# Grouped attention on one Trainium2 core: scores and values of a key tile alternate by halves in TensorE's order

## The chip, the cores and the metric

The program runs on one core of a Trainium2 chip, in one launch. The metric is the device time of that launch in microseconds. A core has a matrix engine (TensorE, PE in the rows, with its weight loads as PEld), a vector engine (DVE), a scalar engine (ACT), GpSimd (POOL) and DMA queues. Each engine runs its own instruction stream in program order; streams meet only through semaphores.

## The reference, cut to what matters

Two layers are computed on `x` (4 x 256 x 512) with a context of 4 x 1601 x 512. Layer 0 is a latent cross attention and an int4 linear layer; layer 1 is the attention below and a mixture of low-rank experts. The change is in the attention of layer 1:

```python
hidden = concatenate([context, latents], axis=1)          # 1601 + 256 = 1857 keys
q = (latents @ Wq.T)   # 16 heads of 96
k = (hidden @ Wk.T)    # 4 key-value heads of 96, each for G = 4 query heads
v = (hidden @ Wv.T)
scores = einsum('bkgqd,bksd->bkgqs', q, k) / sqrt(96)
attn = softmax(scores)
out = einsum('bkgqs,bksd->bkgqd', attn, v) ... @ Wo.T
x = x + out
```

## The kernel before, in words

Four stages follow each other: `context_products`, `latent_attention_and_ffn`, `grouped_attention` and `mixture`. Only the third, `grouped_attention`, is changed. Queries, keys and values come to it through DRAM.

It loops over S = 16 heads s (4 batches x 4 key-value heads). A head has 4 query heads x 256 queries = 1024 query columns, held as two halves of 512 (one PSUM bank each), and KT = 15 key tiles kt of 128 keys, the last of 65. All products are made from a high and a low part, three matmuls each:

- `scores(s, kt)`: for each half, three matmuls into one of SB = 3 score banks (L1435 to L1437). Each bank waits until ACT is done with what stood in it three halves before (`exp_done`).
- ACT, `probs`: for each half two exponentials of the same bank, `ph` (L1530, the high part) and `pf` (L1533, full precision). `pf` waits for POOL to be done with the same half of the tile before.
- POOL subtracts, `pl = pf - ph` (L1366), the low part, once per half.
- `values(s, kt)`: for each half, three matmuls into the output bank of that half (L1452, L1453 with `ph`; L1455 with `pl`). They accumulate over the 15 tiles; at the first tile of the next head they wait for `o_done`, the two copies by which ACT empties both output banks (L1557). ACT issues these copies behind `probs(s + 1, 0)` in its stream, and they wait for the last `values` of head s.

Beside it runs a ring of other work, `ring_item`, in the order that `beside(s)` writes out: for head s + 1 the 32 products of queries and keys whose row maxima DVE takes (L1383, read by L1605), the sum of head s - 1 (L1387, L1607), its 8 output projections (L1394 to L1396, read by L1610), and after each batch a layer norm on DVE (L67 to L82, heads 5, 9 and 13; it has two ring items between its Newton passes L77 to L79) and the first products of the mixture. A ring item takes one of RB = 3 banks and waits until DVE has read what stood there three items before. `fill()` on TensorE issues the next ring item, if there is one left. DVE takes the items in the same order.

The row maxima of head s + 1 are needed before its first scores: at kt = KT - 2, `max_rows(s + 1)` transposes them on TensorE (L1422), DVE writes them into the query operand (`rows_of`, L93), and `scores(s + 1, 0)`, issued at kt = KT - 1, waits for that (`row_done`).

TensorE's order for one key tile is, with S for the scores of the next tile, V for the values of this one, f for a ring item and 0 and 1 for the halves: `S0 f S1 f V0 f V1 f`. In the last three tiles (`late`) no item stands behind V; and S of the last tile is that of the next head's first, without items. The items of a normal head run out at kt = 10, those of heads 5, 9 and 13 at kt = 12; head 15 has none in its first 12 places. The streams of ACT, POOL and DVE are not touched by the change.

Of the kernel before, what the change touches and what calls it, by code (L numbers as in the profile page):

```python
# [14 lines left out]
BANK = 512  # L15
# [8 lines left out]
H1, KV1, HD1 = 16, 4, 96  # L24
# [1157 lines left out]
def grouped_attention(nc, A, ident, negid, ps, ln, q_scr, k_scr, v_scr, x_scr, y_scr, z_scr, wo_scr, w1T, h8all, dlall):  # L1182
# [5 lines left out]
    S = B * KV1  # L1188
    KT = KT1
# [7 lines left out]
    with ExitStack() as ctx:  # L1197
        def sb(name, shape, dt=F32):
            return ctx.enter_context(nc.sbuf_tensor(name, shape, dt))

        def sem(name):
            return ctx.enter_context(nc.semaphore(name))

        kf = sb("kf", [HD1, NK])
        kh = sb("kh", [HD1 + QT, 3, NK + 1], F32R)
        kl = sb("kl", [HD1, 3, NK + 1], F32R)
        vf = sb("vf", [P, KT, HD1])
        vh = sb("vh", [P, 2, KT, HD1 + 1], F32R)
        vl = sb("vl", [P, 2, KT, HD1 + 1], F32R)
        qh = sb("qh", [HD1 + QT, 3, GC], F32R)  # L1210
        ql = sb("ql", [HD1, 3, GC], F32R)
        woT = sb("woT", [HD1, 2, G, D], F32R)
        ph = sb("ph", [P, 2, GC], F32R)
        pl = sb("pl", [P, 2, GC], F32R)
# [22 lines left out]
        s_mm, phi, exp_done, plo = sem("scores1"), sem("probs_hi"), sem("probs1"), sem("probs_lo")  # L1237
        av_mm, o_done, n_done = sem("values1"), sem("o_copied1"), sem("x_normal")
# [3 lines left out]
        OB, M0, RB, SB = 3, 5, 3, 3  # L1242

        def bank(i, n=BANK):
            return ps[:, i * BANK:i * BANK + n]
# [30 lines left out]
        def read(kind, a, i):  # L1276

            return ring_done, ring[kind, a, i] + 1
# [90 lines left out]
        @block.tensor  # L1369
        def _(pe):  # L1370
            def ring_item(kind, a, i):
                n = ring[kind, a, i]
                at = bank(M0 + n % RB)
                if n >= RB:
                    pe.wait_ge(ring_done, n - RB + 1)
                if kind == "max":
                    if i == 0:
                        pe.wait_ge(q_in[a % 3], 32 * (a // 3 + 1))
                    j, ch = i // len(cuts), i % len(cuts)
                    k0, _, k = cuts[ch]  # L1380
                    if j == 0:
                        pe.wait_ge(kh_done, 4 * a + ch + 1)
                    mm = pe.matmul(at[:, 0:k], qh[0:HD1, a % 3, j * P:(j + 1) * P], kh[0:HD1, a % 3, k0:k0 + k],  # L1383
                                   start=True, stop=True)
                elif kind == "sum":
                    pe.wait_ge(sum_in, (a + 1) * 16)
                    mm = pe.matmul(at[:, 0:QT], sums[:, :], ident[0:QT, 0:QT], start=True, stop=True)  # L1387
                elif kind == "out":
                    if i == 0:
                        pe.wait_ge(wo_in, 16 * (a + 1))  # L1390
                        pe.wait_ge(ol_done, a + 1)
                    h, t = i // TT, i % TT
                    cols = slice(h * T + t * P, h * T + (t + 1) * P)
                    pe.matmul(at, oh[:, cols], woT[:, 0, h, :], start=True, stop=False)  # L1394
                    pe.matmul(at, oh[:, cols], woT[:, 1, h, :], start=False, stop=False)
                    mm = pe.matmul(at, ol[:, cols], woT[:, 0, h, :], start=False, stop=True)  # L1396
                elif kind == "turn":
                    if i == 0:
                        pe.wait_ge(n_done, a + 1)
                    for c in range(2):  # L1400
                        for t in range(TT):
                            mm = pe.transpose(at[:, c * T + t * P:c * T + (t + 1) * P],
                                              xn[:, t, (2 * i + c) * P:(2 * i + c + 1) * P], ident[:, :])
                elif kind == "h":
                    if i == 0:
                        pe.wait_ge(*read("turn", a, 1))
                    for c in range(DC):
                        mm = pe.matmul(at, xT[:, c, i * P:(i + 1) * P], w1T[:, c, :], start=(c == 0), stop=(c == DC - 1))
                elif kind == "z":
                    for c in range(DC):  # L1410
                        mm = pe.matmul(at[0:R, 0:T], aw[:, c, :], xT[:, c, :], start=(c == 0), stop=(c == DC - 1))
                elif kind == "h8":
                    for c in range(DC):
                        mm = pe.matmul(at[:, 0:NE], xT[:, c, 1:T:2], w1T[:, c, 0:NE], start=(c == 0), stop=(c == DC - 1))
                else:
                    pe.wait_ge(*read("z", a, 0))
                    mm = pe.matmul(at[:, 0:NE], zb[:, 1:T:2], liT[:, :], start=True, stop=True)
                mm.then_inc(ring_mm, 1)

            def max_rows(s):  # L1420
                pe.wait_ge(mxr_done, s + 1)
                pe.transpose(bank(M0)[0:QT, 0:P], mx[:, :], ident[:, :]).then_inc(row_mm, 1)  # L1422

            def scores(s, kt, fill):
                n = s * KT + kt
                if kt == 0:
                    pe.wait_ge(row_done, s + 1)
                    pe.wait_ge(kl_done, 4 * s + 4)
                k0, m = kt * P, keys[kt]
                for half in range(2):  # L1430
                    if 2 * n + half >= SB:
                        pe.wait_ge(exp_done, 2 * n + half - SB + 1)
                    out = bank((2 * n + half) % SB)[0:m, :]
                    cols = slice(half * BANK, (half + 1) * BANK)
                    pe.matmul(out, kh[:, s % 3, k0:k0 + m], qh[:, s % 3, cols], start=True, stop=False)  # L1435
                    pe.matmul(out, kl[:, s % 3, k0:k0 + m], qh[0:HD1, s % 3, cols], start=False, stop=False)  # L1436
                    mm = pe.matmul(out, kh[0:HD1, s % 3, k0:k0 + m], ql[:, s % 3, cols], start=False, stop=True)  # L1437
                    mm.then_inc(s_mm, 1)
                    if half == 0:
                        fill()  # L1440

            def values(s, kt, fill):
                n = s * KT + kt
                if kt == 0:
                    pe.wait_ge(vl_done, 4 * s + 4)
                    if s:
                        pe.wait_ge(o_done, 2 * s)
                m = keys[kt]
                for half in range(2):
                    out, cols = bank(OB + half)[0:HD1 + 1, :], slice(half * BANK, (half + 1) * BANK)  # L1450
                    pe.wait_ge(phi, 2 * n + half + 1)
                    pe.matmul(out, vh[0:m, s % 2, kt, :], ph[0:m, n % 2, cols], start=(kt == 0), stop=False)  # L1452
                    pe.matmul(out, vl[0:m, s % 2, kt, :], ph[0:m, n % 2, cols], start=False, stop=False)  # L1453
                    pe.wait_ge(plo, 2 * n + half + 1)
                    mm = pe.matmul(out, vh[0:m, s % 2, kt, :], pl[0:m, n % 2, cols], start=False, stop=(kt == KT - 1))  # L1455
                    if half == 0:
                        fill()
                mm.then_inc(av_mm, 1)

            pe.wait_ge(const, 5)  # L1460
            for item in beside(-1):
                ring_item(*item)
            max_rows(0)
            pe.wait_ge(w_small, 48)
            for s in range(S):
                items = iter(beside(s))

                def fill():
                    item = next(items, None)
                    if item:  # L1470
                        ring_item(*item)

                if s == 0:
                    scores(0, 0, lambda: None)
                for kt in range(KT):
                    if kt + 1 < KT:
                        scores(s, kt + 1, fill)
                        fill()
                    elif s + 1 < S:
                        scores(s + 1, 0, lambda: None)  # L1480
                    if s + 1 < S and kt == KT - 2:
                        max_rows(s + 1)
                    late = kt > KT - 4
                    values(s, kt, (lambda: None) if late else fill)
                    if not late:
                        fill()
                assert next(items, None) is None
            for item in beside(S) + last_batch():
                ring_item(*item)
# [349 lines left out]
```

## Time and profile before

| | us |
|---|---|
| runs | 2040.28, 2049.16, 2047.75 (median 2047.75) |
| profiled execution | 2043.46, of it span 2041.7 |
| TensorE busy | 1922.5 (94% of the span) |
| ACT, DVE, POOL busy | 944.3, 1118.8, 653.1 |

The span holds all four stages. Busy time is a sum over the stages, so that what a change in the third is worth has to be read in a timeline of the third. In that, each row is one instruction (or several in a row): start, duration, engine, line, operation, tiles. A matmul's row is longer than the distance to the next one, because they are pipelined; the distance between starts is what it costs. Brackets at a row's end give the idle time of its engine before it and what ended that.

### The profile page before, as it was taken

The numbers are of one execution on the slowest core, as the hardware profiler recorded it, in microseconds if no ns is written. First come the engines' busy times: TensorE is split into PE (matmuls) and PEld (weight loads), VectorE is DVE, ScalarE is ACT, GpSimd is POOL, SyncE is SP. The second block draws the span as 40 slices with busy tenths as digits, with TensorE's granted clock in tenths as the row PEclk, the third lists the DMA queues.
The fourth block names the chain that finished last, engine by engine and source line by source line (L and its number), as shares of the span: only waits on it lengthen the run. The fifth ranks groups of instructions, "written<-read, shape, count | busy, mean of one in ns | idle before, by whom it ended". The sixth has DMA issues, their size and how long they took to land. (4 is left out here: it accounts for less than half of the span.)

```text
span 2041.7 us, 23682 instructions
## 1 busy us (share of the span) xinstructions
PE 1922.5 (94%) x8690; PEld 1368.1 (67%) x8690; DVE 1118.8 (55%) x2093; ACT 944.3 (46%) x1826; POOL 653.1 (32%) x504
## 2 busy tenths in 40 slices
PE   6999998999999999998869999999999999999986
PEld 6999984444555556464637777767777777777752
DVE  1433325666666665652266666666666566664433
ACT  1332322444344334343127666655666466665640
POOL 0000000000000000000028777756776577765740
PEclk9999995999899999999769999999999999999996
DMA  5556733000111010010261232213222222212112
GB/s 176 157 170 204 226 121 70 1 11 17 50 34 42 31 42 27 11 52 26 80 167 45 75 85 75 60 30 86 74 72 75 76 79 62 56 49 57 31 31 97
DMA packets 109697, 149.51 MB, mean 73 GB/s; under 512 B 28777, under 2 KB 87529, under 8 KB 106510
## 3 DMA queue, kind: packets, MB, share of 16 engines
q1 hardware_dynamic: 101630, 145.36, 24.9%
q10 hardware_dynamic: 7952, 2.64, 0.6%
q8 instruction: 69, 1.13, 0.2%
q14 instruction: 46, 0.38, 0.1%
HBM read 96.52 MB, written 51.39 MB: 72 GB/s over the span
## 5 line engine op out<-in xcount | busy, mean ns | idle before, releaser
L1366 POOL TENSOR_TENSOR pl<-pf,ph 128x512 fp32r<-128x512 f32 (+1 forms) x480 | 640.9, 1352 | 300.9 <-ACT pf L1533 299.2
L1530 ACT ACTIVATE ph<-ps 128x512 fp32r<-128x512 f32 (+1 forms) x480 | 288.5, 601 | 352.8 <-PE ps L1437 351.8
L1605 DVE TENSOR_REDUCE pm<-ps 128x1 f32<-128x464 f32 (+1 forms) x512 | 317.9, 635 | 119.9 <-PE ps L1383 113.5
L1132 DVE TENSOR_REDUCE pm<-ps 128x1 f32<-128x400 f32 (+1 forms) x512 | 264.2, 567 | 103.1 <-PE ps L970 100.2
L1031 ACT ACTIVATE pr<-ps 128x512 f32<-128x512 f32 (+1 forms) x416 | 219.4, 602 | 194.3 <-PE ps L909 193.0
L1533 ACT ACTIVATE pf<-ps 128x512 f32<-128x512 f32 (+1 forms) x480 | 289.2, 603 | 0.2 <-POOL pl L1366 0.2
L1355 POOL MEMSET vf<- 128x96 f32 x1 | 0.2, 178 | 711.2 <-POOLq L685 711.2
L1383 PE MATMUL ps<-kh,qh 96*128 96x464 f32 (+1 forms) x512 | 199.6, 399 | 21.9 <-DMA ql<-q_scr 12.9
L922 PE MATMUL ps<-pr,cv 128*64 128x512 f32 (+1 forms) x832 | 208.1, 616 | 0.0
L1435 PE MATMUL ps<-qh,kh 104*128 104x512 f32 (+1 forms) x480 | 194.7, 406 | 1.4 <-issue 1.4
L1452 PE MATMUL ps<-ph,vh 128*97 128x512 f32 (+1 forms) x480 | 194.3, 405 | 0.0
L1436 PE MATMUL ps<-qh,kl 96*128 96x512 f32 (+1 forms) x480 | 191.0, 398 | 0.0
L970 PE MATMUL ps<-cst,ast 96*128 96x400 f32 (+1 forms) x512 | 175.5, 402 | 16.4 <-DVE pm L1132 12.2
L1437 PE MATMUL ps<-ql,kh 96*128 96x512 f32 (+1 forms) x480 | 189.6, 395 | 0.0
L1455 PE MATMUL ps<-pl,vh 128*97 128x512 f32 (+1 forms) x480 | 189.1, 394 | 0.4 <-POOL pl L1366 0.3
L1453 PE MATMUL ps<-ph,vl 128*97 128x512 f32 (+1 forms) x480 | 189.0, 394 | 0.0
L970 PEld LDWEIGHTS ps<-cst,ast 96*128 96x128 f32 x512 | 96.6, 201 | 110.7 <-DVE pm L1132 45.6
L909 PE MATMUL ps<-ast,cst 104*128 104x512 f32 (+1 forms) x416 | 153.2, 431 | 5.5 <-ACT pr L1031 2.0
L1383 PEld LDWEIGHTS ps<-kh,qh 96*128 96x128 f32 x512 | 99.5, 195 | 62.8 <-DVE pm L1605 22.4
L1610 DVE SCALAR_TENSOR_TENSOR x<-ps,rec,x 128x512 f32<-128x512 f32 x128 | 95.5, 748 | 69.6 <-PE ps L1396 69.0
L922 PEld LDWEIGHTS ps<-pr,cv 128*64 128x64 f32 (+1 forms) x832 | 51.7, 138 | 85.9 <-issue 59.2
L1435 PEld LDWEIGHTS ps<-qh,kh 104*128 104x128 f32 (+1 forms) x480 | 89.3, 186 | 29.6 <-DVE qh L93 5.8
(222 smaller groups left out, 2648.8 us busy)
## 6 DMA issues: line engine op xcount, KB each, us to landing
woT<-wo_turned SPq DMA_DIRECT2D x16, 1536.0 KB, 9.2
cnat<-in_ctx_dram SPq DMA_DIRECT2D x16, 768.0 KB
q_scr<-qst SPq DMA_DIRECT2D x48, 256.0 KB, 2.4
kf<-k_scr SPq DMA_DIRECT2D x16, 696.4 KB, 4.8
vf<-v_scr SPq DMA_DIRECT2D x16, 672.0 KB
v_scr<-vst SPq DMA_DIRECT2D x64, 144.0 KB, 2.3
k_scr<-kst SPq DMA_DIRECT2D x36, 192.0 KB, 4.7
wo_turned<-wo_out SPq DMA_DIRECT2D x32, 192.0 KB, 2.8
```

The costliest lines, as they stand in the source:

```text
L922: mm = pe.matmul(bank(OB)[64 * half:64 * half + 64, :], cv[0:keys[kt], b % 2, kt, :], pr[0:keys[kt], n % NPR, half * BANK:(half + 1) * BAN ...
L970: mm = pe.matmul(out[:, 0:k], ast[0:HD1, grp * GC + j * P:grp * GC + (j + 1) * P], cst[0:HD1, b % 2, k0:k0 + k], start=True, stop=True)
L1031: act.activation(pr[0:keys[kt], n % NPR, half * BANK:(half + 1) * BANK], bank((2 * n + half) % SB)[0:keys[kt], :], ACT.Exp, scale=S0).then ...
L1132: dve.reduce_max(pm[:, j, ch:ch + 1], src[:, 0:cuts[ch][1]], AX).then_inc(done["dve"], 1)
L1366: pool.tensor_tensor(pl[0:m, n % 2, cols], pf[0:m, half, :], ph[0:m, n % 2, cols].bitcast(F32), ALU.subtract).then_inc(plo, 1)
L1383: mm = pe.matmul(at[:, 0:k], qh[0:HD1, a % 3, j * P:(j + 1) * P], kh[0:HD1, a % 3, k0:k0 + k], start=True, stop=True)
L1435: pe.matmul(out, kh[:, s % 3, k0:k0 + m], qh[:, s % 3, cols], start=True, stop=False)
L1436: pe.matmul(out, kl[:, s % 3, k0:k0 + m], qh[0:HD1, s % 3, cols], start=False, stop=False)
L1452: pe.matmul(out, vh[0:m, s % 2, kt, :], ph[0:m, n % 2, cols], start=(kt == 0), stop=False)
L1530: act.activation(ph[0:keys[kt], n % 2, cols], src, ACT.Exp, scale=S1).then_inc(phi, 1)
L1533: act.activation(pf[0:keys[kt], half, :], src, ACT.Exp, scale=S1).then_inc(exp_done, 1)
L1605: ins = dve.reduce_max(pm[:, j, ch:ch + 1], at[:, 0:cuts[ch][1]], AX)
```

## The change

In `scores` and `values` the loop over halves goes out: each call now does one half. The loop over halves stands in TensorE's main loop, so that the order of a key tile becomes `S0 f V0 f S1 f V1 f`; in the late tiles `S0 f V0 S1 f V1`, and at the last tile `S0 V0 S1 V1`, where S is the next head's. `max_rows` comes between S1 and V1 of tile KT - 2, where it stood between S1 and V0. The waits keep their places in front of the half to which they belong: `row_done` in front of S0 of a head's first tile, `o_done` (both copies) in front of V0 of its first tile. The number and the order of the ring items, and all the instructions, are the same.

```diff
-            def scores(s, kt, fill):
+            def scores(s, kt, half):
                 n = s * KT + kt
-                if kt == 0:
+                if kt == 0 and half == 0:
                     pe.wait_ge(row_done, s + 1)
                     pe.wait_ge(kl_done, 4 * s + 4)
...
-            def values(s, kt, fill):
+            def values(s, kt, half):
                 n = s * KT + kt
-                if kt == 0:
+                if kt == 0 and half == 0:
                     pe.wait_ge(vl_done, 4 * s + 4)
                     if s:
                         pe.wait_ge(o_done, 2 * s)
...
                 if s == 0:
-                    scores(0, 0, lambda: None)
+                    for half in range(2):
+                        scores(0, 0, half)
                 for kt in range(KT):
-                    if kt + 1 < KT:
-                        scores(s, kt + 1, fill)
-                        fill()
-                    elif s + 1 < S:
-                        scores(s + 1, 0, lambda: None)
-                    if s + 1 < S and kt == KT - 2:
-                        max_rows(s + 1)
                     late = kt > KT - 4
-                    values(s, kt, (lambda: None) if late else fill)
-                    if not late:
-                        fill()
+                    for half in range(2):
+                        if kt + 1 < KT:
+                            scores(s, kt + 1, half)
+                            fill()
+                        elif s + 1 < S:
+                            scores(s + 1, 0, half)
+                        if s + 1 < S and kt == KT - 2 and half == 1:
+                            max_rows(s + 1)
+                        values(s, kt, half)
+                        if not late:
+                            fill()
```

## Rows read from the trace of the kernel before

**Rows 1.** Windows: stretch, busy (count) of PE, PEld, DVE, ACT, POOL; clock, DMA.

```profile
1056.10:1984.50 928.40, 915.76 (x3918) 687.63 (x3918) 555.76 (x864) 578.76 (x1124) 640.89 (x480) 0.99 0.24 63
...
1339.00:1397.00 58.00, 56.27 (x237) 40.08 (x238) 34.88 (x62) 27.73 (x55) 28.55 (x24) 1.00 0.21 58
```

**Rows 2.** Waits of the weight loads, third stage: us in total, times, longest.

```profile
PEld ps L1383 <- DVE pm L1605: 11.1, 9, 1.8
...
PEld ps L1435 <- DVE qh L93: 5.8, 15, 0.4
```

**Rows 3.** Timeline around a transpose of the row maxima, head 0 to 1.

```profile
1106.18 0.28 PE L1422 MATMUL ps<-ident,mx 128*8 128x128 f32 x1
...
1106.50 1.22 DVE L93 TENSOR_TENSOR qh<-ps,negid 8x1024 fp32r<-8x1024 f32 x1 [8.91 <-PE ps L1422]
...
1107.44 0.40 PE L1455 MATMUL ps<-pl,vh 128*97 128x512 f32 x1
1107.77 0.19 PEld L1435 LDWEIGHTS ps<-qh,kh 104*128 104x128 f32 x1 [0.39 <-DVE qh L93]
1107.77 0.51 PE L1435 MATMUL ps<-qh,kh 104*128 104x512 f32 x1
...
1108.11 0.40 PE L1436 MATMUL ps<-qh,kl 96*128 96x512 f32 x1
...
1108.35 0.40 PE L1437 MATMUL ps<-ql,kh 96*128 96x512 f32 x1
```

**Rows 4.** The same timeline, to the next head's first values.

```profile
1109.81 0.60 ACT L1530 ACTIVATE ph<-ps 128x512 fp32r<-128x512 f32 x1
...
1110.29 0.62 ACT L1533 ACTIVATE pf<-ps 128x512 f32<-128x512 f32 x1
1110.43 0.39 PE L1455 MATMUL ps<-pl,vh 65*97 65x512 f32 x1
...
1110.86 1.07 ACT L1557 COPY o<-ps 97x512 f32<-97x512 f32 x2
...
1111.36 0.37 PE L1383 MATMUL ps<-kh,qh 96*128 96x464 f32 x1
...
1111.56 0.40 PE L1435 MATMUL ps<-qh,kh 104*128 104x512 f32 x1
...
1111.82 0.61 ACT L1530 ACTIVATE ph<-ps 128x512 fp32r<-128x512 f32 x1
...
1112.47 0.40 PE L1452 MATMUL ps<-ph,vh 128*97 128x512 f32 x1
```

**Rows 5.** Lines L93 and L1557 in the whole trace: count, duration ns min/median/max.

```profile
L93 DVE TENSOR_TENSOR qh<-ps,negid x16: 1216/1218/1219, 1056.6 to 1920.2; 8x1024 fp32r<-8x1024 f32 x16
...
L1557 ACT COPY o<-ps x32: 585/586/592, 1110.9 to 1972.8; 97x512 f32<-97x512 f32 x32
```

**Rows 6.** Timeline, the last key tile of head 15: scores to values.

```profile
1967.58 0.40 PE L1437 MATMUL ps<-ql,kh 96*65 96x512 f32 x1
...
1968.07 0.59 ACT L1530 ACTIVATE ph<-ps 65x512 fp32r<-65x512 f32 x1 [0.72 <-PE ps L1437]
...
1968.57 0.58 ACT L1533 ACTIVATE pf<-ps 65x512 f32<-65x512 f32 x1
...
1969.22 2.53 POOL L1366 TENSOR_TENSOR pl<-pf,ph 65x512 fp32r<-65x512 f32 x2 [0.24 <-ACT pf L1533]
...
1970.57 0.47 PE L1455 MATMUL ps<-pl,vh 65*97 65x512 f32 x1
```

**Rows 7.** Costliest groups of the page: POOL's subtraction.

```profile
L1366 POOL TENSOR_TENSOR pl<-pf,ph 128x512 fp32r<-128x512 f32 (+1 forms) x480 | 640.9, 1352 | 300.9 <-ACT pf L1533 299.2
```

**Rows 8.** Timelines of POOL, DVE and PE in the layer norm of head 5.

```profile
1333.22 2.53 POOL L1366 TENSOR_TENSOR pl<-pf,ph 128x512 fp32r<-128x512 f32 x2 [0.45 <-ACT pf L1533]
...
1333.56 0.97 DVE L77 TENSOR_TENSOR ln_t<-ln_y 128x2 f32<-128x2 f32 x1
1334.56 1.21 DVE L78 SCALAR_TENSOR_TENSOR ln_u<-ln_t,ln_v 128x2 f32<-128x2 f32 x1
...
1340.11 0.48 PE L1383 MATMUL ps<-kh,qh 96*128 96x466 f32 x1 [1.32 <-DVE pm L1605]
...
1340.70 0.16 DVE L78 SCALAR_TENSOR_TENSOR ln_u<-ln_t,ln_v 128x2 f32<-128x2 f32 x1
```

More of the change, by code:

```diff
@@ L1429, in scores @@
                 k0, m = kt * P, keys[kt]
[L1430 to L1439, printed above, removed]
-                        fill()
-            def values(s, kt, fill):
+                if 2 * n + half >= SB:
+                    pe.wait_ge(exp_done, 2 * n + half - SB + 1)
+                out = bank((2 * n + half) % SB)[0:m, :]
+                cols = slice(half * BANK, (half + 1) * BANK)
+                pe.matmul(out, kh[:, s % 3, k0:k0 + m], qh[:, s % 3, cols], start=True, stop=False)
+                pe.matmul(out, kl[:, s % 3, k0:k0 + m], qh[0:HD1, s % 3, cols], start=False, stop=False)
+                mm = pe.matmul(out, kh[0:HD1, s % 3, k0:k0 + m], ql[:, s % 3, cols], start=False, stop=True)
+                mm.then_inc(s_mm, 1)
+            def values(s, kt, half):
                 n = s * KT + kt
-                if kt == 0:
+                if kt == 0 and half == 0:
                     pe.wait_ge(vl_done, 4 * s + 4)
@@ L1448, in values @@
                 m = keys[kt]
[L1449 to L1456, printed above, removed]
-                        fill()
-                mm.then_inc(av_mm, 1)
+                out, cols = bank(OB + half)[0:HD1 + 1, :], slice(half * BANK, (half + 1) * BANK)
+                pe.wait_ge(phi, 2 * n + half + 1)
+                pe.matmul(out, vh[0:m, s % 2, kt, :], ph[0:m, n % 2, cols], start=(kt == 0), stop=False)
+                pe.matmul(out, vl[0:m, s % 2, kt, :], ph[0:m, n % 2, cols], start=False, stop=False)
+                pe.wait_ge(plo, 2 * n + half + 1)
+                mm = pe.matmul(out, vh[0:m, s % 2, kt, :], pl[0:m, n % 2, cols], start=False, stop=(kt == KT - 1))
+                if half == 1:
+                    mm.then_inc(av_mm, 1)
             pe.wait_ge(const, 5)
@@ L1473, in _ @@
                 if s == 0:
-                    scores(0, 0, lambda: None)
+                    for half in range(2):
+                        scores(0, 0, half)
                 for kt in range(KT):
-                    if kt + 1 < KT:
-                        scores(s, kt + 1, fill)
-                        fill()
-                    elif s + 1 < S:
-                        scores(s + 1, 0, lambda: None)
-                    if s + 1 < S and kt == KT - 2:
-                        max_rows(s + 1)
-                    late = kt > KT - 4
-                    values(s, kt, (lambda: None) if late else fill)
-                    if not late:
-                        fill()
+                    late = kt > KT - 4
+                    for half in range(2):
[9 more added lines that the diff above has]
+                            fill()
                 assert next(items, None) is None
```

## The prediction

> **What bounds the kernel now.** I first read the windows by stage. The third stage takes 928.4 us and TensorE is busy for 915.8 of it at a granted clock of 0.99; ACT, DVE and POOL are busy for 579, 556 and 641 [rows 1]. So the stage runs at TensorE's own pace. Next come the waits, which say what is left to gain: the weight loads waited 11.1 us in nine places for DVE's maxima, all in the three layer norms, and 5.8 us in 15 places, once per change of head, for the rows that DVE writes [rows 2]. Then I read the timeline at a change of head, because a new order can cost only where a wait has little cover in front of it.
>
> The unit of all that follows is a step: three matmuls of one half, S or V. From the third matmul of the new head's S0 (1108.35) to the third of the last V1 (1110.43) lie three steps, 2.08 us [rows 3, 4]; a step is 0.69 us and one matmul 0.23. A ring item of one matmul is 0.20 (1111.36 to 1111.56) [rows 4].
>
> **The change part by part.**
>
> *What is the same.* Instructions, ring items and their order are equal on every engine, so TensorE's work gains or loses nothing: in the rows one step follows another at 0.23 us whether it is S after V or V after S. Only the distance between an instruction and the one that waits for it changes.
>
> *A step fewer behind the transpose.* The transpose (L1422) starts at 1106.18, DVE starts the rows at 1106.50 and takes 1.22, so S0 of the next head is let go at 1107.72 and starts at 1107.77, 0.05 later. TensorE was ready at 1107.44 + 0.23 = 1107.67 [rows 3]. It loses 0.10 now, with two V steps (V0 and V1 of tile 13) as cover. After the change only V1 stands between them. TensorE is ready at 1107.67 - 0.69 = 1106.98, the rows come when they came, and the wait is 0.79. That is 0.69 more. L93 runs 16 times, the first of them at the stage's start [rows 5]: 15 x 0.69 = 10.4 us. What is queued behind the waiting S0 is V0 of the last tile, which is ready and can't pass it. DVE can't start the rows sooner in relation to the transpose, so both ends of this term are close: 15 x 0.60 to 15 x 0.75, 9.0 to 11.3.
>
> *A step fewer in front of the emptied output banks.* V0 of a head's first tile waits for both copies (L1557). Before, V1 of the last tile is followed by `S0 f S1 f`; after, by `S0 f` alone. Count from A, the start of the third matmul of the new head's S0 (1108.35 in the rows):
> - TensorE, new order: V0, S1, V1, S0 f, V0. The third matmul of S1 starts at A + 2 x 0.69 = A + 1.38, that of V1 at A + 2.07, and V0 of the new head could start at A + 2.07 + 0.23 + 0.69 + 0.20 = A + 3.19.
> - ACT: S1's exponentials stand in front of the copies. `ph` starts 0.49 after the third matmul (1967.58 to 1968.07) [rows 6], at A + 1.87; `pf` 0.48 later, A + 2.35; the copies 0.57 after that (1110.29 to 1110.86), A + 2.92; they take 1.07 [rows 4], A + 3.99, and with 0.05 for the release A + 4.04.
> - So TensorE waits 0.85. Before, V0 started at 1112.47, A + 4.12, and the copies were done at 1111.93: no wait, 0.5 to spare [rows 4]. The new S1 comes a step later, and that makes the copies later too; the lost cover is not all.
> - A weight load that waits is no longer hidden: behind the wait for the rows the next matmul starts 0.34 later and not 0.23 (1107.77 to 1108.11) [rows 3]. That is 0.11 more, for this wait alone, since the other has it already. 0.96 per change of head, 15 x 0.96 = 14.4 us. Lower end: were the copies held only by V1 (0.43 behind its third matmul, 1110.43 to 1110.86), they would be done at A + 3.57, and the wait is 0.43 + 0.11: 8.1 us. Upper end: `pf` held up by another 0.5 us by POOL: 21.9 us. I take 14.4, because ACT runs strictly in its order.
>
> On the 0.11: the load of S0's weights starts with its matmul, at the release [rows 3]. The Trainium skill (TensorE: Matmul & The Clock Gate, Step-by-step: what each phase is for) says that TensorE pulls weight loads ahead of matmuls still in flight. By that rule the 0.11 would be hidden and the sum be 1.7 us less; by the rows a load that carries the wait itself is not pulled past it, and I keep the 0.11.
>
> *The chain S, ACT, POOL, V inside a head.* In rows 6 it is exposed: third matmul of S at 1967.58, `pf` at 1968.57, POOL at 1969.22 for 1.27 each, and V's third matmul at 1970.57. It needs 2.99 us. In the new order without ring items V's third matmul stands 0.23 + 4 x 0.69 + 0.46 = 3.45 behind S's, so 0.46 is to spare; with four items 1.3. Before it was a step more, less what POOL's second half waited behind the first (1.27 - 0.69). POOL needs 2.54 per tile of 2.76 at least. I count nothing for it. Ends: 0, and +10 if POOL's delays by DVE (its mean is 1352 ns against 1265 undisturbed [rows 6, 7]) come together in the 75 tiles without items. At head 15, 0.2 because no item stands in front of the wait, and at its end 0.1 for the last S1, a step later: 0.3.
>
> *The layer norms of heads 5, 9, 13.* Here the change can give something back. DVE's Newton passes on 128 x 2 elements take 0.16 where POOL is idle (1340.70), but L77 took 0.97 and L78 1.21 beside POOL's pair of subtractions from 1333.22, and L78 ends at 1335.77 with the pair's end 1335.75 [rows 8]. Each waited for the end of one POOL instruction. Such delays make TensorE wait for the ring, as at 1340.11; in all 11.1 us by the weight loads [rows 2], some 9.6 beyond the hidden part of loads. The new order sends S0 and S1 out 1.8 us apart in tiles with items, so POOL's subtractions come singly with 0.5 between them, and L77 to L79 (0.16 + 0.2 + 0.2) can run in one gap: a pass then costs about 1.0 and not 2.4, for two of three passes. But DVE also starts them 0.96 later, since the second item stands behind the wait for the copies. I take 1.6 us per layer norm, 5 us in all; ends 0 and 9.6.
> The Trainium skill (SBUF — State Buffer, Terms) says that DVE and GpSimd share a port pair that one of them holds for a whole instruction while the other is blocked. By that rule the trace agrees: 0.97 and 1.21 end with POOL's instructions.
>
> *The clock.* The window of head 5 has TensorE idle for 1.7 us in pieces up to 1.32 and a granted clock of 1.00 [rows 1, 8], so pauses below 1 us should cost no clock: 0.
>
> *The sum.* 10.4 + 14.4 + 0.3 - 5.0 = +20.1 us. The profiled execution took 2043.46 (span 2041.7 and 1.8 around it): 2063.6. The median of the runs shown, 2047.75, is 4.3 higher, which gives 2067.9. I take 2066, between them. With all lower ends it is 9.0 + 8.1 - 9.6 = +7.5, with all upper ones 11.3 + 21.9 + 10.3 = +43.
>
> **The rivals.**
> 1. *Only the row wait counts.* The copies are hidden after all (a release of the first copy is not enough, since V0 waits for both, but the wait for `row_done` has delayed everything and ACT may catch up): 10.4 + 0.3 - 5.0 = +5.7, 2052. Against it: A is counted behind that wait already.
> 2. *The chain becomes the bound.* In tiles without items POOL is busy 92% of the time; each such tile 0.15 to 0.2 late gives 75 x 0.18 = +13 on top of 20, 2079. For it: DVE's two-input operations hold POOL up. Against it: 0.46 to spare.
> 3. *No change.* 10.4 us for the rows, the copies hidden and the layer norms' whole 9.6 given back: +1, 2047.
> 4. *Faster.* ACT's and POOL's work, spread evenly, ends the ring's waits in the layer norms: -9.6 us, 2037. It decides only if both waits at the change of head stay below 0.64 us together (9.6 / 15); by the rows they are 1.65. It could be so if DVE wrote the rows in less than 0.6 us, and it takes 1.22 each time [rows 5].
>
> **How the numbers follow.** Forecast 0.67 (alone: 2056 to 2076), rival 1 0.09, rival 2 0.12, rival 3 0.08, rival 4 0.04. About 0.5%, 10 us, is what a measurement can tell from no change. Slower: 0.67 + 0.12 and a small part of rival 1, in all 0.83, since in the cases of +7.5 to +10 some of the forecast's own range falls away; same 0.13; faster 0.04. The range that holds 8 in 10 goes from rival 1 to rival 2: 2053 to 2079.
>
> **What would show it.** Step one: the waits list `L1435 <- DVE qh L93` with 15 x (0.39 + 0.69), about 16 us. Step two: a new entry in that list, `L1452 <- ACT o L1557`, 15 times, about 1 us each. Chain: `L1455 <- POOL pl` stays below 3 us. Layer norm: L78's mean falls, and `L1383 <- DVE pm` goes from 11.1 towards 6. The third stage grows to about 948 us, the others stay. Wrong would be: no entry for L1557, or large waits of L1455, or a granted clock below 0.99 in the third stage.

## Result, and the profile after

| | us |
|---|---|
| kernel before | 2047.75 (median of 5, 2040.28 to 2050.49) |
| changed kernel | 2056.92 (median of 5, 2054.58 to 2057.39) |
| ratio | 1.0047, 95% interval 1.0025 to 1.0068 |
| profiled execution | 2054.81, span 2053.0 |

The kernel became 9.2 us slower. The direction was forecast. The time was forecast at 2066 and lies 0.9 us above the lower end of the range from 2056 to 2076; the size, 20.1 us by the sum, is twice what these medians show.

The waits of the changed kernel's weight loads in the third stage (us in total, times, longest); `L1434` is the first matmul of S, `L1448` that of V:

```profile
PEld ps L1434 <- DVE qh L93: 16.1, 15, 1.1
PEld ps L1448 <- issue: 15.0, 18, 1.2
...
PEld ps L1383 <- DVE pm L1602: 5.1, 3, 1.7
```

The wait for the rows has grown from 5.8 to 16.1 us, that for the maxima in the layer norms has fallen from 11.1 to 5.1 [rows 2], and 15 waits before V's first matmul are new (this matmul had 11 waits of 3.0 us in all before, and has 18 of 15.0). The profile puts these down to "issue". What ended them is in the timeline of the first change of head (start, duration, engine, line, tiles):

```profile
1101.40 0.27 PE L1422 MATMUL ps<-ident,mx 128*8 128x128 f32 x1
...
1101.71 1.22 DVE L93 TENSOR_TENSOR qh<-ps,negid 8x1024 fp32r<-8x1024 f32 x1 [8.37 <-PE ps L1422]
...
1102.98 0.50 PE L1434 MATMUL ps<-qh,kh 104*128 104x512 f32 x1 [0.62 <-DVE qh L93]
...
1105.63 0.39 PE L1451 MATMUL ps<-pl,vh 65*97 65x512 f32 x1
...
1105.86 0.59 ACT L1530 ACTIVATE pf<-ps 128x512 f32<-128x512 f32 x1
...
1106.34 1.08 ACT L1554 COPY o<-ps 97x512 f32<-97x512 f32 x2
...
1106.56 0.37 PE L1383 MATMUL ps<-kh,qh 96*128 96x464 f32 x1
...
1107.51 0.45 PE L1448 MATMUL ps<-ph,vh 128*97 128x512 f32 x1 [0.58 <-issue]
...
1107.80 0.39 PE L1449 MATMUL ps<-ph,vl 128*97 128x512 f32 x1
```

S0 starts 1.58 behind the transpose (1.59 before [rows 3]), but with one step less of work between. V0 could start at 1106.56 + 0.21 = 1106.77. The copies end at 1106.34 + 1.08 = 1107.42, and V0 starts at 1107.51, 0.74 late.

**A ruler for heads.** From one row of L93 to the next is one head; 16 rows give 15 intervals. Before, such an interval is 55.05 us on average in the 11 heads without a layer norm (55.0 to 55.1) and 69.41, 69.39, 69.38 in the three with one. After, it is 56.50 (56.4 to 56.6), and 69.22, 69.15, 69.09. The fifteenth interval, the last, is shorter: 49.9 before, 50.8 after. From the first row of L93 to the end of the span it is 985.1 us before (from 1056.56) and 1002.0 after (from 1050.96): +16.9 us. The unchanged part ahead of it was 5.6 us shorter in the changed kernel's trace; its granted clock over the first 1050 us is 0.94 there and 0.93 in the first trace of before.

**Why the times differ by less than the third stage.** I traced the kernel before once more (r0 below). The first trace (2043.46) shows no drop of the clock in the layer norms; the second, of 2045.79, does. Three windows of six microseconds in the first layer norm, and one in the second, kernel before, second trace (columns as in the first group of rows ahead of the prediction):

```profile
1331.00:1337.00 6.00, 4.26 (x18) 2.79 (x18) 5.72 (x13) 2.52 (x6) 2.88 (x3) 1.00 0.00 0
1337.00:1343.00 6.00, 5.37 (x17) 3.45 (x15) 4.30 (x9) 2.50 (x5) 2.51 (x2) 0.72 0.00 0
1343.00:1349.00 6.00, 6.00 (x27) 4.79 (x28) 4.63 (x8) 4.12 (x9) 2.87 (x3) 1.00 0.00 0
...
1574.00:1584.30 10.30, 9.77 (x24) 6.91 (x25) 5.59 (x10) 4.22 (x9) 4.89 (x4) 0.50 0.00 0
```

The same execution's matmuls there, behind the pauses of 1.33 and 0.63:

```profile
1335.71 0.48 PE L1383 MATMUL ps<-kh,qh 96*128 96x466 f32 x1 [1.33 <-DVE pm L1605]
...
1338.43 0.68 PE L1383 MATMUL ps<-kh,qh 96*128 96x464 f32 x1 [0.63 <-DVE pm L1605]
1338.91 0.63 PE L1452 MATMUL ps<-ph,vh 128*97 128x512 f32 x1
1339.33 0.63 PE L1453 MATMUL ps<-ph,vl 128*97 128x512 f32 x1
...
1342.12 0.40 PE L1435 MATMUL ps<-qh,kh 104*128 104x512 f32 x1
```

The distance is 0.43 and not 0.23: the lower of the clock's two levels, 1.2 GHz, for some 3.4 us here and in the third layer norm, and for 10.2 us in the second. The three heads with a layer norm took 70.95, 73.77 and 70.74 in that execution, 7.3 us more than in the first trace. The changed kernel's layer norms have one pause for the maxima each and show a clock of 1.00:

```profile
1327.68:1396.90 69.22, 66.82 (x282) 47.68 (x281) 45.67 (x78) 37.62 (x72) 39.03 (x31) 1.00 0.21 57
```

That this decides the times can be read from executions that were timed and not traced, because each has its granted clock over the whole span. The kernel before was timed 76 times beside the experiments. In 30 executions the clock was 0.953 or more, and their median is 2039.0 (2036.8 to 2044.3); in 43 it was 0.951 or less, and their median is 2048.1 (2042.9 to 2053.5); three at 0.952 lie between, at 2042.5 to 2042.9. Beside r0 the two groups stand apart (12 at 2037 to 2042, 20 at 2045 to 2054), in another batch times between them occur too. All five executions of the changed kernel have 0.954 and lie within 3 us. So the change costs 18 us against the executions of before with the higher clock, near the 16.9 of the traces, and 9 us against the others, which are the majority. The five executions of before in the table of results have no clock on record. Where in an untraced execution the clock was lost isn't recorded; in the trace of r0 it was in the layer norms.

### The profile page after: what moved, and what is told of

The parts are those of the page before. It is cut to its first block and busy times, and to the rows that moved or that the text cites. A ratio compares the mean times of both kernels' runs of the same rounds, so it can differ in the third digit from the quotient of the medians.

```text
span 2053.0 us, 23682 instructions
## 1 busy us (share of the span) xinstructions
PE 1919.3 (93%) x8690; PEld 1363.1 (66%) x8690; DVE 1124.5 (55%) x2093; ACT 962.5 (47%) x1826; POOL 636.2 (31%) x504
## 3 DMA queue, kind: packets, MB, share of 16 engines
q8 instruction: 69, 1.13, 0.2%
## 5 line engine op out<-in xcount | busy, mean ns | idle before, releaser
L1366 POOL TENSOR_TENSOR pl<-pf,ph 128x512 fp32r<-128x512 f32 (+1 forms) x480 | 623.9, 1300 | 334.8 <-ACT pf L1530 330.1
L1530 ACT ACTIVATE pf<-ps 128x512 f32<-128x512 f32 (+1 forms) x480 | 284.3, 592 | 0.0
L1434 PE MATMUL ps<-qh,kh 104*128 104x512 f32 (+1 forms) x480 | 195.9, 408 | 10.6 <-DVE qh L93 9.2
L1448 PE MATMUL ps<-ph,vh 128*97 128x512 f32 (+1 forms) x480 | 193.6, 403 | 8.8 <-issue 8.8
L1451 PE MATMUL ps<-pl,vh 128*97 128x512 f32 (+1 forms) x480 | 189.3, 394 | 0.6 <-POOL pl L1366 0.4
L1383 PEld LDWEIGHTS ps<-kh,qh 96*128 96x128 f32 x512 | 99.7, 195 | 56.4 <-DVE pm L1602 16.4
L1434 PEld LDWEIGHTS ps<-qh,kh 104*128 104x128 f32 (+1 forms) x480 | 89.5, 186 | 43.8 <-DVE qh L93 16.1
```

The source lines that it names most:

```text
L1366: pool.tensor_tensor(pl[0:m, n % 2, cols], pf[0:m, half, :], ph[0:m, n % 2, cols].bitcast(F32), ALU.subtract).then_inc(plo, 1)
L1530: act.activation(pf[0:keys[kt], half, :], src, ACT.Exp, scale=S1).then_inc(exp_done, 1)
```

## The experiments

All intervals are from L93 to L93 in one traced execution of each kernel, to be held against 55.05 (before) and 56.50 (changed) for the heads without a layer norm. The ratios are to the kernel before, timed anew beside each group of experiments, and so carry its two groups of executions; the intervals don't.

**e1: the transpose one half earlier.**

```diff
-                        if s + 1 < S and kt == KT - 2 and half == 1:
+                        if s + 1 < S and kt == KT - 2 and half == 0:
                             max_rows(s + 1)
```

> The changed kernel with the transpose of the row maxima one half earlier, in front of V0 of tile KT - 2 instead of V1: three steps of 0.69 us stand between it and the next head's S0, where DVE needs 1.59. The interval is that between two rows instructions of DVE (L93) in heads without a layer norm: 55.05 us before, 56.50 in the changed kernel. Theory (two waits at each change of head): the wait for L93 vanishes whole, 0.69 that the change added and 0.21 that was there before, so the interval falls to 55.60 and the kernel is 13.5 us faster than the changed one, about 2 us faster or slower than before. Rival (the alternation costs something in every tile, and the wait is only where it is seen): the next wait takes its place, the interval stays above 56.2.

Measured: 55.62, no wait for L93 left in the list, 2042.55 us; ratio to before 0.9996 (0.9978 to 1.0013). 15 x 0.88 = 13 us went with this wait: 0.69 each that the change had added, and 0.2 that the kernel before had too.

**e2: the old order in the first tile.**

```diff
+                    if kt == 0:
+                        for half in range(2):
+                            scores(s, kt + 1, half)
+                            fill()
+                        for half in range(2):
+                            values(s, kt, half)
+                            fill()
+                        continue
```

> The changed kernel with the old order S0 f S1 f V0 f V1 f in the first tile of each head only. Theory: V0 of a new head again has a step more in front of it, the wait for the emptied output banks (0.80 us in the changed kernel's trace) vanishes, the interval falls from 56.50 to 55.70, 15 x 0.80 = 12 us in all; the wait for L93 stays at 1.1. Rival as in the first run: the interval stays above 56.2.

Measured: 55.72, and the entry for `L1448` fell from 15.0 to 1.0 us: the theory holds. But the kernel is slower, 2064.32 us, ratio 1.0103 (1.0071 to 1.0135), because the heads with a layer norm took 75.2, 75.1 and 75.2. Each has a pause of TensorE of 2.5 us, and the clock is low behind it; in the first:

```profile
1342.00:1352.00 10.00, 9.10 (x22) 6.72 (x23) 5.75 (x10) 2.63 (x5) 2.56 (x3) 0.51 0.00 0
```

**e6: a step less in the order of before.**

```diff
-                    if s + 1 < S and kt == KT - 2:
-                        max_rows(s + 1)
                     late = kt > KT - 4
-                    values(s, kt, (lambda: None) if late else fill)
+                    rows = (lambda: max_rows(s + 1)) if s + 1 < S and kt == KT - 2 else (lambda: None)
+                    values(s, kt, rows if late else fill)
```

> The kernel before, with its own order everywhere, and only the transpose of the row maxima moved behind V0 of tile KT - 2, so that one step less covers it. Theory: this alone costs 0.69 at each change of head, interval 55.05 to 55.74, heads with a layer norm 69.4 to 70.1, in all +10.3 us on the kernel before, and no wait for the output banks appears. Rival (the cost of the row wait in the changed kernel comes from the alternation): interval below 55.3.

Measured: 55.75 and the wait for L93 at 16.1 us, the changed kernel's to the tenth; 2053.38 us, ratio 1.0042 (1.0022 to 1.0062). The heads with a layer norm took 70.1 twice, as forecast, and 71.64 in the first, where the clock was low for 3.4 us behind pauses of 1.31 and 0.64. The row wait belongs to the transpose's place and not to the alternation.

**e8: Newton passes with one tensor input, in the kernel before.**

```diff
+        if single:
+            for step in (lambda c: dve.tensor_scalar(t[:, c], y[:, c], y[:, c], None, ALU.mult),
+                         lambda c: dve.tensor_scalar(u[:, c], t[:, c], -0.5, v[:, c], ALU.mult, ALU.mult),
+                         lambda c: dve.tensor_scalar(y[:, c], u[:, c], 1.5, y[:, c], ALU.add, ALU.mult)):
+                chain.mark(step(slice(0, 1)))
+                chain.link(step(slice(1, 2)))
+            continue
         chain.link(dve.tensor_tensor(t[:, :], y[:, :], y[:, :], ALU.mult))
...
-                          ln["y"], pause).then_inc(n_done, 1)
+                          ln["y"], pause, single=True).then_inc(n_done, 1)
```

> The kernel before, with the three Newton passes of the layer norm in this stage written as operations with one tensor input and a per-partition factor, one column at a time: six instructions a pass and not three. Theory A (POOL holds up only operations of DVE with two inputs from SBUF): no instruction takes above 0.3 us, a pass takes about 1.2 us and not 2.4, the heads with a layer norm go from 69.4 to some 67.5, in all -5 us. Theory B (POOL holds up these small ones too): passes beside POOL's pair still take 2.4 us or more, no gain. Either way the heads without a layer norm stay at 55.05.

POOL and the first pass in its trace:

```profile
1328.96 2.55 POOL L1373 TENSOR_TENSOR pl<-pf,ph 128x512 fp32r<-128x512 f32 x2 [0.46 <-ACT pf L1540]
...
1329.28 0.33 DVE L78 TENSOR_SCALAR ln_t<-ln_y 128x1 f32<-128x1 f32 x2
1329.64 0.33 DVE L79 TENSOR_SCALAR ln_u<-ln_t,ln_v 128x1 f32<-128x1 f32 x2
1330.01 0.33 DVE L80 TENSOR_SCALAR ln_y<-ln_u,ln_y 128x1 f32<-128x1 f32 x2
```

Beside POOL's pair two instructions take 0.33 us together, where one with two inputs took 0.97 and 1.21 [rows 8]. Theory A: 67.36, 67.27 and 67.24 for the heads with a layer norm, 55.05 for the others, 2032.43 us, ratio 0.9946 (0.9926 to 0.9966). That is more than the 5 us forecast: 6.3 us by the intervals, and beyond them the drops of the clock, which its executions don't have (0.953 or 0.954 in all seven).

**e3: both repairs of the order.** The diffs of e1 and e2 together.

> Both repairs at once: the alternation, with the transpose one half earlier and the old order in the first tile of each head. Theory: both waits gone, interval 56.50 - 0.90 - 0.80 = 54.80, 0.25 below the kernel before (the 0.21 of the old row wait among it); heads with a layer norm 69.2 - 1.7 = 67.5 against 69.4 before, if the first tile's old order does not take the layer norm's gain away. In all 12 x -0.25 and 3 x -1.9, some 8 us faster than before. Rival (the alternation costs something in every tile): interval 55.05 or above.

Measured: 54.83 for the other heads, as forecast, but 71.7, 74.3 and 74.3 for those with a layer norm: 2048.03 us, ratio 1.0023 (1.0006 to 1.0039). My reading that the layer norm's gain would stay was wrong. DVE and TensorE in the first layer norm:

```profile
1327.44 1.25 DVE L77 TENSOR_TENSOR ln_t<-ln_y 128x2 f32<-128x2 f32 x1
1328.73 1.22 DVE L78 SCALAR_TENSOR_TENSOR ln_u<-ln_t,ln_v 128x2 f32<-128x2 f32 x1
...
1333.34 1.21 DVE L77 TENSOR_TENSOR ln_t<-ln_y 128x2 f32<-128x2 f32 x1
...
1334.98 1.95 DVE L82 TENSOR_SCALAR xn<-x,ln_mv,ln_y 128x512 f32<-128x512 f32 x2
...
1337.53 0.76 PE L1383 MATMUL ps<-kh,qh 96*128 96x464 f32 x1 [2.50 <-DVE pm L1610]
1338.09 0.63 PE L1434 MATMUL ps<-qh,kh 104*128 104x512 f32 x1
```

With the first tile in the old order DVE meets a pair of POOL in the first pass again, and a single instruction of POOL in the last pass and in L82. TensorE stands for 2.5 us, and its next matmuls are 0.43 apart. The window behind the pause:

```profile
1337.50:1341.00 3.50, 3.47 (x9) 2.69 (x10) 2.26 (x4) 1.39 (x3) 0.23 (x1) 0.51 0.00 0
```

**e4: the copies in front of S1's exponentials on ACT.**

```diff
-            def probs(s, kt):
+            def probs(s, kt, halves=(0, 1)):
...
-                for half in range(2):
+                for half in halves:
...
                 if s + 1 < S:
-                    probs(s + 1, 0)
+                    probs(s + 1, 0, (0,))
                 act.wait_ge(av_mm, (s + 1) * KT)
...
+                if s + 1 < S:
+                    probs(s + 1, 0, (1,))
```

> The changed kernel, and on ACT the two copies that empty the output banks stand in front of the exponentials of the next head's S1, and no longer behind them. Theory (ACT's order makes the copies late): they start 0.43 behind the third matmul of the last V1 and not 0.71, TensorE's wait falls from 0.74 to about 0.46, the interval from 56.50 to 56.2. Rival (the copies are late by the last V1 alone): no change, 56.50.

Measured: 56.29, a gain of 0.21 from ACT's order (0.28 forecast). V waits for `pl` in 16 places, 5.2 us by its weight loads, where it did in 3. Heads with a layer norm 76.2, 73.2 and 73.1, each with a pause of 2.6 us and the low clock behind it; 2069.65 us, ratio 1.0128 (1.0102 to 1.0154). Why the copies' place lengthens these pauses wasn't followed up.

**e4s: each half waits for its own copy.**

```diff
-                if kt == 0 and half == 0:
-                    pe.wait_ge(vl_done, 4 * s + 4)
+                if kt == 0:
+                    if half == 0:
+                        pe.wait_ge(vl_done, 4 * s + 4)
                     if s:
-                        pe.wait_ge(o_done, 2 * s)
+                        pe.wait_ge(o_done, 2 * s - 1 + half)
```

> The changed kernel, where V0 of a head's first tile waits only for the copy of its own output bank, and V1 for the second. Theory: the first copy is done 0.49 earlier, so the wait falls from 0.74 to 0.25 and the interval from 56.50 to 56.0; V1 does not wait. Rival (another thing, such as the probabilities, ends V0's wait): no change.

Measured: 56.01 and 68.7, 2049.20 us, ratio 1.0029 (1.0015 to 1.0043). With e4 and e2 it shows that the wait the profile calls "issue" is the one for the copies: their place on ACT, how many are waited for and a step more in front of V0 each move it near to what was forecast.

**e5: all repairs on the pure alternation** (e1, e4 and e4s).

> The pure alternation with all three repairs: transpose one half earlier, copies first on ACT, one wait for each output bank. Theory: first copy done 0.43 + 0.59 + 0.05 = 1.07 behind the last third matmul, V0 is ready at 1.12, so no wait: interval 54.80, heads with a layer norm 67.5, some 8 us faster than before. Rival: the later exponentials of S1 make the low part late (pl), waits of L1451 appear and the interval stays above 55.0.

Measured: 55.38, and the rival: waits for POOL's `pl` of 13.7 us in 18 places against 1.9 in the changed kernel. Heads with a layer norm 72.3 to 73.8, with pauses of 2.6 us; 2053.99 us, ratio 1.0054 (1.0034 to 1.0075). In its trace the copies start 0.43 behind V's last third matmul (1159.82 to 1160.25), and V0 then waits for the low part:

```profile
1159.82 0.39 PE L1452 MATMUL ps<-pl,vh 65*97 65x512 f32 x1
1160.25 1.07 ACT L1555 COPY o<-ps 97x512 f32<-97x512 f32 x2 [0.95 <-PE ps L1452]
...
1162.39 3.79 POOL L1366 TENSOR_TENSOR pl<-pf,ph 128x512 fp32r<-128x512 f32 x3 [1.72 <-ACT pf L1531]
...
1163.72 0.48 PE L1452 MATMUL ps<-pl,vh 128*97 128x512 f32 x1 [0.28 <-POOL pl L1366]
```

**r0: the kernel before again.**

> The kernel before, unchanged, as one more execution with a trace: how much the stages that the change does not touch differ between executions. Theory: the third stage repeats to 0.1 us a head (interval 55.05, heads with a layer norm 69.4), while the time up to the first row of L93, 1056.6 in the first trace and 1050.7 to 1056.3 in nine others, moves by some us; ratio 1.00. Rival: the changed kernels have a faster first part for a reason in their code, and this run again shows 1056.

Measured: 55.05 once more, 2046.62 us, ratio 1.0014 (0.9992 to 1.0035), and the first row of L93 at 1052.29. So the first part moves by itself. That the heads with a layer norm repeat was wrong: 70.95, 73.77 and 70.74, with the rows of the clock above.

**f1: e3 with the layer norm of e8.**

> The alternation with the transpose one half earlier, the old order in the first tile of each head, and the layer norm's Newton passes with one tensor input. Theory: interval 54.80 as with the two repairs alone; the heads with a layer norm, 74.3 there with a pause of 2.5 us and the half clock behind it, fall to 67.0 (67.3 of the kernel before with this layer norm, less 0.25); the clock stays at 1.00; about 17 us faster than the kernel before. Rival: the long pauses come from the order and not from the Newton passes, and the heads with a layer norm stay above 70.

Measured: 54.82, heads with a layer norm 67.57, 67.50 and 67.41, one pause of 1.2 us in each and no low clock, 2032.38 us, ratio 0.9946 (0.9926 to 0.9966). The Newton passes, the only difference from e3, were the cause of the long pauses.

**f2: the order of before, repaired.** The layer norm of e8, and:

```diff
+                    rows = s + 1 < S and kt == KT - 2
                     if kt + 1 < KT:
-                        scores(s, kt + 1, fill)
+                        scores(s, kt + 1, (lambda: max_rows(s + 1)) if rows else fill)
+                        if rows:
+                            fill()
                         fill()
...
-                    if s + 1 < S and kt == KT - 2:
-                        max_rows(s + 1)
```

> The order of the kernel before, with the transpose one half earlier and the same layer norm: everything of the run beside it but the alternation. Theory (the alternation is worth nothing by itself once both waits and the layer norm are dealt with): interval 55.05 - 0.21 = 54.84, heads with a layer norm 67.1, the two runs equal within 0.1%. Rival (evenly spread halves help in every tile): this one is slower by 0.2 us a head or more.

Measured: 54.86, heads with a layer norm 67.20, 67.11 and 67.03, 2031.90 us, ratio 0.9938 (0.9917 to 0.9960). It beats both kernels and equals f1 within 0.1%, by the intervals of the heads without a layer norm within 0.04 us. In the tiles that f1 alternates the alternation is worth nothing. Against e8 (2032.43) the earlier transpose shows in the intervals, 0.2 a head, and hardly in the times.

**f3: the changed kernel with the layer norm of e8.**

> The changed kernel with the layer norm's Newton passes with one tensor input. Theory (the change's gain in the layer norm and this one are the same gain, POOL's hold on DVE): the heads without a layer norm stay at 56.50; those with one go from 69.2 to 68.8, that is 67.3 + 1.45 for the change of head, and not to 69.2 - 2.1 = 67.1 as they would if the gains added.

Measured: 56.49 and 69.22, 69.08, 69.07, 2057.32 us, ratio 1.0072 (1.0044 to 1.0101). Even the 0.4 that I gave it did not come: the one pause left, 1.22, ends where the changed kernel's ends. So the two gains don't add: they are one.

## Why the prediction was right or wrong, point by point

- **The row wait, 0.69 per change of head: right.** 16.1 us in the list where "about 16" was named, S0 1.58 behind the transpose; e1 takes it away, e6 makes it alone.
- **The wait for the copies: mechanism right, size off.** 0.96 was forecast; the timeline has 0.74 and 0.06 behind it, 0.80, 2.4 us less over 15. I took 0.57 from `pf` to the copies [rows 4], but there V1's end held them; behind ACT's own work alone it is 0.48 (1105.86 to 1106.34). `ph` of S1 started 0.43 and not 0.49 behind its third matmul, and the exposed load costs 0.06 for V and not 0.11. That the list would name `ACT o L1557` was wrong, it says "issue". Both waits come to 1.49; the intervals show 1.45.
- **The chain S, ACT, POOL, V: right.** `L1451` waits 1.9 us for POOL; before, L1455 waited 1.8. Rival 2 is out. Only with the copies in front on ACT was the margin used up: 5.2 us in e4, 13.7 in e5.
- **The layer norms, -5.0: right.** The three intervals fall by 0.24 on average though each holds a change of head worth 1.45: 3 x 1.69 = 5.1 us. DVE's passes show why; these are POOL and DVE in the changed kernel:

```profile
1334.46 1.29 POOL L1366 TENSOR_TENSOR pl<-pf,ph 128x512 fp32r<-128x512 f32 x1 [0.68 <-ACT pf L1530]
...
1335.22 0.55 DVE L77 TENSOR_TENSOR ln_t<-ln_y 128x2 f32<-128x2 f32 x1
1335.80 0.16 DVE L78 SCALAR_TENSOR_TENSOR ln_u<-ln_t,ln_v 128x2 f32<-128x2 f32 x1
```

L77 waits for POOL's single instruction and the other two fit into the gap; a pass takes 0.94 where it took 2.4. Three pauses (0.41, 1.32 and 0.62) became one of 1.21. One loss wasn't in the forecast. L82, which ran undisturbed before, now waits for POOL as well, and the pause that is left ends behind it:

```profile
1341.10 1.13 DVE L82 TENSOR_SCALAR xn<-x,ln_mv,ln_y 128x512 f32<-128x512 f32 x2
...
1340.16 2.16 DVE L82 TENSOR_SCALAR xn<-x,ln_mv,ln_y 128x512 f32<-128x512 f32 x2
...
1342.92 0.48 PE L1383 MATMUL ps<-kh,qh 96*128 96x464 f32 x1 [1.21 <-DVE pm L1602]
```

(The first row is the kernel before, the others the changed one.) The first two passes save 1.47 and 1.35, the third and L82 lose 0.2 and 1.0: 1.6 in all. The forecast's 1.6 came from another loss, the later start of the passes; so it is partly luck that the size agrees.
- **The clock at nothing: this step failed.** I read "a window with pauses up to 1.32 has a clock of 1.00" [rows 1, 8] as a property of the kernel; it was one of that execution. In the second trace of before the same pauses were followed by the low level. For the pauses that the change adds, some 0.6 at each change of head, the zero was right: the clock is 1.00 there. But the change takes two of three pauses in each layer norm away, and with them the drops, and that is a gain that the sum did not have: 7.3 us by that trace, 9 us by the medians of the two groups of executions. The third stage was forecast at +20.1 and is +16.9 against an execution without drops. That the drops take half of this back in the medians rests on the granted clocks of all 76 executions and on two traces of before. Rivals 3 and 4 had this sign, but the wrong place: the boundary waits came nearly whole.
- **The time in the range: partly luck.** The forecast started from 2043.46 and from 2047.75. The first holds a slow first part (5.6 us more than the changed kernel's trace), the second the drops in the layer norms. 2043.46 + 16.9 - 5.6 = 2054.8 is the traced time of the changed kernel. The 20.1 was 3.2 too much and the starting point some 6, and 2056.92 is just inside.

## What to carry to other kernels

When an order is made finer, count for every semaphore how much work still lies between its giver and its waiter: a steady state that hides everything says nothing about the seams, and here two steps less at a seam cost 1.45 us each time while the tiles gained nothing. Pauses of one or two microseconds can cost more than themselves through the clock, in some executions only, so read more than one trace, and the granted clocks of the timed executions, before a clock is put at zero. And look at small two-input operations of one engine beside a long one of POOL: a few of them held up a tuned matmul stream, and rewriting them brought more than any order tried here.

## What the runs showed of the hardware

- DVE's instructions with two inputs from SBUF waited for the end of POOL's subtraction even on 2 elements a partition (0.97 and 1.21 us against 0.16); the same arithmetic with one tensor and a per-partition factor took 0.16 each beside it. L82, one tensor input of 512 elements, did wait: 1.95 for two beside POOL against 1.13. The Trainium skill (SBUF — State Buffer, SBUF: two separate sides) has both: a DVE operation in a two-port mode, or one with two SBUF inputs against a GpSimd operation that reads SBUF, and the GpSimd operation exclude each other for a whole instruction. The traces agree for the two-input operations; that L82 ran in a two-port mode no row shows, only that it waited.
- TensorE's clock fell to its lower level for 3.4 us behind a pause of 0.63 that followed one of 1.33 in one execution of the kernel before, and did not in another with the same pauses. Over the 14 traces, by layer norm of this stage: where the longest pause was 2.5 or 2.6 us (e2, e3, e4, e5) the clock was low in or behind it in 12 of 12, for 3.4 to 10.2 us; where pauses of 0.4, 1.3 and 0.6 followed each other 2.7 to 3.4 us apart (before, r0, e6), in 4 of 9; where the longest was a single one of 1.2, with at most the 0.6 of the change of head beside it (changed, e1, e4s, f1, f3), in none of 15; with one of 0.8 (e8, f2), in none of 6.
- The low level cost 1.4 to 1.5 us for 3.4 us of it and 4.4 for 10.2 (the intervals of r0 against those of the first trace).
